# Sixteen-head attention steps: another order for the turned groups, and one copy moved from VectorE to ScalarE

## The reference, cut to what matters

```
scores = (q @ k.T) / sqrt(8)          # 128 queries x K keys; K = 120 (L1) or 128 (MLA)
scores = where(mask, -big, scores)    # a key mask in L1, causal in MLA
attn   = softmax(scores)              # over the keys
out    = attn @ v                     # 8 channels for each head, 16 heads side by side
y      = out.reshape(128, 128) @ w_o  # then the residual is added
```

## Time and profile before

| | |
|---|---|
| median of three runs | 1278.69 us |
| the profiled execution, its own time | 1280.42 us |
| its span, first to last instruction | 1278.9 us |
| TensorE matmul busy | 1221.2 us (95%) |
| VectorE busy | 936.8 us (73%) |
| ScalarE busy | 797.5 us (62%) |
| GpSimd busy | 585.1 us (46%) |
| mean granted TensorE clock | 0.981 |

### The profile page before, as it was taken

One profiled execution on the slowest core, in us unless ns is written; L12 is line 12 of the kernel. 1 busy time (PEld: TensorE's weight loads), 2 busy tenths in 40 slices (PEclk: granted clock), 3 DMA queues, 4 the chain that ended last, 5 costly groups with the idle time before them and its releaser, 6 DMA issues.

```text
span 1278.9 us, 38214 instructions
## 1 busy us (share of the span) xinstructions
PE 1221.2 (95%) x13719; PEld 874.3 (68%) x13719; DVE 936.8 (73%) x2049; ACT 797.5 (62%) x2101; POOL 585.1 (46%) x675
## 2 busy tenths in 40 slices
PE   4899999999999995998999999999999989999996
PEld 1566666666666664447888788788888767777774
DVE  7767766777667764579999999999999965344331
ACT  2687788878877783225877787767666733333331
POOL 5476666566665663414333423353233234333442
PEclk9999999999999998998999999999999999999998
DMA  9000000000000000000000002000000000000000
GB/s 225 14 2 2 0 0 0 0 0 0 0 0 0 1 1 5 0 0 12 10 10 10 11 8 72 3 4 1 0 0 0 1 1 9 9 8 8 8 16 10
DMA packets 22742, 14.74 MB, mean 12 GB/s; under 512 B 6378, under 2 KB 21610, under 8 KB 22540
## 3 DMA queue, kind: packets, MB, share of 16 engines
q1 hardware_dynamic: 22520, 13.75, 4.3%
q10 hardware_dynamic: 148, 0.01, 0.0%
HBM read 11.66 MB, written 2.10 MB: 11 GB/s over the span
## 4 chain that ended last, share of the span: by engine, by line
PE 40%; issue 10%; POOL 5%; DVE 3%; POOLq 0%; ACT 0%; DVEq 0%
PE psum L1580 10%; PE psum L1591 5%; PE psum L1567 5%; POOL pair_acc L2310 4%; PE psum L1594 4%; PE psum L998 2%; PE psum L2090 2%; PE psum L2100 2%; PE psum L1005 2%; PE psum L1562 2%; PE psum L1546 1%; PE psum L1548 1%; PE psum L1547 1%; PE psum L1602 1%; POOL pair_acc L2304 1%
## 5 line engine op out<-in xcount | busy, mean ns | idle before, releaser
L715 POOL TENSOR_TENSOR r_norm<-ssm,mhalf 128x24 f32<-128x24 f32 x32 | 134.9, 4215 | 156.9 <-DVE ssm L619 156.8
L1948 POOL TENSOR_TENSOR pair_QX<-pair_qT,own_slots 128x512 f32<-128x512 f32 x64 | 66.6, 1040 | 248.4 <-ACT pair_qT L1679 236.0
L2156 ACT ACTIVATE pair_hid<-psum 128x512 f32<-128x512 f32 x128 | 76.4, 597 | 141.3 <-PE psum L2090 141.3
L1580 PE MATMUL psum<-ident,pair_probs 128*120 128x128 f32 (+1 forms) x1024 | 153.9, 283 | 0.4 <-ACT pair_probs L1694 0.2
L541 ACT ACTIVATE l_probs<-psum,l_n_max 128x248 f32<-128x248 f32 x256 | 117.2, 482 | 57.9 <-DVE l_n_max L637 57.9
L2310 POOL TENSOR_TENSOR pair_acc<-pair_acc,pair_prod 128x512 f32<-128x512 f32 x64 | 81.2, 1269 | 140.0 <-DVE pair_prod L2269 140.0
L1694 ACT ACTIVATE pair_probs<-psum,pair_n_max 128x120 f32<-128x120 f32 (+1 forms) x512 | 137.7, 380 | 10.8 <-DVE pair_n_max L1748 5.7
L2100 PEld LDWEIGHTS psum<-w,pair_hid 128*128 128x128 f32 x1024 | 123.1, 192 | 26.8 <-issue 26.8
L2269 DVE TENSOR_TENSOR pair_prod<-psum,pair_combine 128x512 f32<-128x512 f32 x64 | 44.2, 691 | 129.7 <-PE psum L2100 129.5
L1515 ACT COPY pair_probsT<-psum 120x512 f32<-120x512 f32 (+1 forms) x128 | 78.7, 615 | 84.7 <-PE psum L1580 84.7
L1580 PEld LDWEIGHTS psum<-ident,pair_probs 128*120 128x120 f32 (+1 forms) x1024 | 109.4, 140 | 31.1 <-ACT pair_probs L1694 12.3
(11 more groups left out here) (294 smaller groups left out, 2922.9 us busy)
## 6 DMA issues: line engine op xcount, KB each, us to landing
X<-x_in SPq DMA_DIRECT2D x8, 256.0 KB, 6.2
out_dram<-pair_acc SPq DMA_DIRECT2D x32, 64.0 KB, 1.5
CT<-ctx_in SPq DMA_DIRECT2D x8, 240.0 KB, 6.6
pair_cT<-ctxT_in SPq DMA_DIRECT2D x32, 60.0 KB, 1.8
w<-w_in SPq DMA_DIRECT2D x1, 1024.0 KB, 5.4
wm<-wm_in SPq DMA_DIRECT2D x1, 768.0 KB, 7.3
wp<-wp_in SPq DMA_DIRECT2D x1, 768.0 KB, 8.7
wkv<-wkv_in SPq DMA_DIRECT2D x1, 512.0 KB, 5.0
```

What stands on the lines that cost most here:

```text
L715: pool.tensor_tensor(r_norm[:, :], ssm[:, :], mhalf[:, 0:3 * H], ALU.pow).then_inc(s["norm_inverted"], 1)
L1580: tr = pe.transpose(psum[0:K, 4 + g % 2, j * P:(j + 1) * P], probs[par][:, 4 * g + j, 0:K], ident[:, :])
```

## The change

TensorE's order becomes: turn the input of n+1; project n-2; turn group 3 of n-1; project q, k, v; turn group 2 of n-1; multiply groups 0, 1, 2, 3 of n-1; search totals; scores of n+1; turn group 1 of n; turn group 0 of n. So across the end of a step the four turned groups 1, 0, 3, 2 follow each other, and nothing is turned between the products.

ScalarE copies group 1 too, which VectorE copied. The exponentials of heads 0 to 7 move from the end of `body(n-1)` to `body(n)` in two halves; between the halves stand the copy of q of n+1 and the copy of group 2 of n-1.

VectorE loses the copy of group 1. Its copy of group 3 moves from before the projection's addition to behind `shift_b`, and `shift_b` now follows `max_b` at once; the statistics come after the copy.

```diff
 # TensorE, body(n)
-                    turn_group(n - 1, 1 - par, 3, l1)
                     if not (early and n == -1):
                         turn_input(n + 1)
                     if not (isinstance(n, int) and n == PAIR + 1):
                         project(n - 2, l1)
-                    turn_group(n - 1, 1 - par, 2, l1)
+                    turn_group(n - 1, 1 - par, 3, l1)
                     if isinstance(n, int) and n == PAIR:
                         pe.wait_ge(a_exp_done, PAIR)
                         moe["turn_first"](pe)
                     project_qkv(n + 1, 1 - par, l1)
+                    turn_group(n - 1, 1 - par, 2, l1)
...
                     multiply_v(n - 1, 1 - par, 0, l1)
                     multiply_v(n - 1, 1 - par, 1, l1)
-                    turn_group(n, par, 1, l1)
                     multiply_v(n - 1, 1 - par, 2, l1)
                     multiply_v(n - 1, 1 - par, 3, l1)
...
                     scores(n + 1, 1 - par, l1)
                     if early and n == -1:
                         find_logits()
+                    turn_group(n, par, 1, l1)
                     turn_group(n, par, 0, l1)
 # ScalarE
-                def exp_a(n, par, l1):
+                def exp_a(n, par, l1, some):
                     if there(n):
                         K = keys(n, l1)
                         wait(act, max_a_taken, n + 1)
                         wait(act, turned[1], n - 1)
-                        for h in range(8):
+                        wait(act, turned[0], n - 1)
+                        for h in some:
...
-                        e.then_inc(a_exp_done, 1)
+                        if some.stop == 8:
+                            e.then_inc(a_exp_done, 1)
 # ScalarE, body(n)
+                    exp_a(n, par, l1, range(0, 4))
                     copy_q(n + 1)
                     copy_group(act.copy, act, n - 1, 2, l1)
+                    exp_a(n, par, l1, range(4, 8))
                     copy_k(n + 1, 1 - par, l1)
...
+                    copy_group(act.copy, act, n, 1, l1)
                     copy_group(act.copy, act, n, 0, l1)
-                    exp_a(n + 1, 1 - par, l1)
 # VectorE, body(n)
                         copy_input(dve, n + 1, l1)
-                    copy_group(dve.tensor_copy, dve, n - 1, 3, l1)
...
                     add_projection(n - 2, l1)
                     max_b(n, par, l1)
+                    shift_b(n, par, l1)
+                    copy_group(dve.tensor_copy, dve, n - 1, 3, l1)
                     take_stats(n - 2, l1)
-                    shift_b(n, par, l1)
...
-                    copy_group(dve.tensor_copy, dve, n, 1, l1)
                     copy_values(dve.tensor_copy, dve, n + 1, 1 - par, l1)
```

## The result

The changed kernel takes 1293.54 us in the median of four runs (1293.49 to 1294.72); the kernel before, run beside it, 1279.61 (1275.88 to 1281.24, four runs). The ratio is 1.0117, with a 95% interval of 1.0098 to 1.0135: slower by 1.2%, where 0.4% was forecast. The profiled execution's span went from 1278.9 to 1291.9 us, +13.0.

A forecast was written before the change was run, and what follows sets the result against it. Two routes of one length, VectorE's and TensorE's, were taken to bound the MLA step. It grows from 6.76 to 6.90 us: +4.5 in 32 steps, L1 nothing, edges +0.3; +4.8 on 1278.69 gives 1283.5, range 1273 to 1295.

The forecast's parts named there:

- steps 2 to 5 of the sum: MLA step from `max_b` through group 3's copy and product 3 to `max_a`: 1.24, 1.12, 0.73, 0.78, 0.21, 0.98, 0.21 us.
- the 0.03 that the prediction added because two routes must be in: At `max_a`, VectorE's and TensorE's routes must both have arrived: 0.03 us added, taking the MLA step from 6.87 to 6.90.
- the wide range: Whole kernel's time, for 8 in 10: 1273 to 1295 us.
- the range of the forecast's own mechanism: Whole kernel's time if VectorE's wait for product 3 sets the step: 1278 to 1291 us, chance 0.64.
- the edges: Steps 17 (search's extra VectorE work, at most -0.6 us) and 64 (group 2's turn delayed, at most +1.1): +0.3 together.
- the addition's 0.26 in step 1: MLA step: VectorE's addition starts 0.26 us after the input copy, which starts 1.14 after `max_a`; `max_b` follows 0.20 later.
- Totals lengthen TensorE's route by 0.28 before and after alike: L1 steps with the search's totals: 0.28 us longer than other L1 steps, unaffected by the change, so L1 costs nothing.
- A free wait on the own engine: VectorE, `shift_b` behind `max_b`: waiting costs nothing, 0.11 us less in 64 steps, -7.0, giving 1276.5 us; chance 0.07.
- TensorE's run binds: TensorE's own work sets the step, 6.37 us MLA and 6.32 L1: -0.39 in 64 steps, -25, giving 1254; chance 0.15.
- ScalarE late: ScalarE's second half of the exponentials delays the bias: 0.24 us in 64 steps, +15 on the forecast, 1299; chance 0.11.
- The clock: TensorE rests about 0.5 us a step and its granted clock falls: at 0.85, +0.6 in 64 steps, about 1322; chance 0.03.

The follow-up runs named there:

- the first experiment: Changed kernel with VectorE's copy of group 3 moved between `max_b` and `shift_b`: 1278.54 us, ratio 1.0002 to the kernel before.

## Why the prediction was right in kind and short in size

- **What takes the step over: right.** `shift_b` at 1.25 behind `max_b` (forecast 1.24), 0.73 from group 3's copy to product 3, 0.78 to `copy_values`, then 0.21, 0.98, 0.21: as in steps 2 to 5 of the sum but for `shift_b`, 1.14 where 1.12 was forecast. `copy_values` waits 0.64 for L1594, the weight loads 0.67 for VectorE's copy; 0.6 and 0.5 were forecast. That the written-out step hits 6.90 is in part luck: the 0.03 that the prediction added because two routes must be in is not seen (VectorE goes on from `copy_values` at its own cost), and 0.01 of `max_b` and 0.02 of `shift_b` stand in its place.
- **The size.** 1293.54 lies inside the wide range but outside the range of the forecast's own mechanism, 1278 to 1291: +4.8 was forecast and +13.9 measured. The two failures below come to 3.2 and 6.6 of step time, and the edges gave 1.8 back.
- **What failed in the MLA: the addition's 0.26 in step 1.** I took it from the row of group 3's copy, which followed the input copy there; the addition stood behind that 0.60 copy, where nothing of its own lateness could show. In looped steps it starts 0.36 behind the input copy (mean; 911.70 - 911.35 = 0.35 above), the input copy 0.03 later than forecast and `max_b` 0.01: about 0.15 in 22 steps, 3.2 us. The 0.03 lay open in the trace of before: the input copy started 1.19 behind `max_a` in every second looped step there, and the prediction read one with 1.14. Written-out steps have 0.26 and 6.90. The last loop written out gives these 0.15 back, and the L1 steps show 6.81 and 6.70 in the same way. A looped addition's row shows no sizes of its inputs and a written-out one does, so its place in X comes from the loop's counter; whether that makes it late was not tried by itself. Why a looped instruction issues late stays open.
- **What failed in L1: "Totals lengthen TensorE's route by 0.28 before and after alike".** The prediction followed ScalarE for the scores, but not the third trial, which the totals need and which stands behind all that the change put on ScalarE. It ends at 658.10 + 0.23 = 658.33, and the totals start at 658.38. 15 steps, +6.6 us. The experiment with the early trial gives 4.8 of it back; the rest is the loop's lateness, and with the loops written out too the steps are back at 6.98.
- **Edges, too small**: the two steps of the search's extra work gained 1.8 where at most 0.6 was allowed. In the first (8.39 to 7.65) VectorE rests nowhere in the trace of before, so the copy taken off it counts there. The second (9.31 to 8.23) gained at least in part for a reason that the prediction does not have. TensorE's wait for the input copy there, before and after, and the stretch behind it before (columns as in the earlier trace rows):

```profile
709.81 0.49 PE L1546 MATMUL psum<-pair_zT,l_wq 128*128 128x128 f32 x2 [1.36 <-DVE pair_zT L1506]
```

```profile
713.09 0.49 PE L1546 MATMUL psum<-pair_zT,l_wq 128*128 128x128 f32 x2 [0.91 <-DVE pair_zT L1506]
```

```profile
711.00:712.00 1.00, 1.00 (x24) 0.92 (x26) 1.00 (x3) 1.00 (x4) 1.00 (x2) 0.50 0.00 0
```

  Behind the rest of 1.36 the granted clock fell to 0.50, the lower level, and group 1's turn and the products ran in that stretch; after the change it stayed at 1.00 through this step. What the clock cost there and what the order cost was not separated.
- **The rivals.** A free wait on the own engine: `shift_b` starts 0.03 behind the end of `max_b` (911.91 + 1.22 to 913.16), and filling that place gave 0.13. The Trainium skill, "VectorE: DVE Perf Modes", section "The DRAIN you can't avoid", measured no extra cost for a semaphore behind each of eight copies; the trace disagrees here too. TensorE's run binds: its condition, an early copy of group 3, is the first experiment, and it takes ScalarE's order as well to come near (6.55, not 6.37). ScalarE late: it came, but through the third trial and the totals and not through the exponentials that the rival names; 7.43 - 6.98 = 0.45 in 15 steps, the loop's part included. The clock: 1.00 over the MLA stretch, although TensorE's weight loads rest 0.67 in each step. The Trainium skill, "TensorE: Matmul & The Clock Gate", section "A second HAM failure mode: psum-queue depth-cycling", tells of a kernel in which short rests between matmul groups made the clock swing; no run here shows that for these steps.

## What to carry to other kernels

When a copy is moved so that an engine hands work over and next needs it back, its whole trip is on the path, and work taken off that engine was worth nothing here wherever it had to wait; move the copy up until other work covers the trip. When work is put on an engine, follow everything queued behind it to its own readers, the rare ones too: the steps with totals, 15 in one half, lost as much as 22 looped steps of the other. Take a price from a row with the same predecessor and, where steps are both looped and written out, from the same kind of step.

## What the runs showed of the hardware

A step run by the loop took 7.03 to 7.06 where the same step written out took 6.90, and 6.81 where it took 6.70. Before the change both kinds took about 6.75; there the addition followed the 0.60 copy. Behind `max_b`'s 1.21 the looped step is nearly as short as the written-out one, too (6.77 and 6.84 against 6.77), so a longer instruction ahead seems to cover the late issue. A VectorE instruction that reads the one right before it starts 0.03 behind its end, where one that does not starts 0.08 before; an independent instruction between them gave 0.13 of a step back. TensorE's granted clock fell to 0.50 behind one rest of 1.36 in the kernel before and behind one of 1.36 in the kernel with all steps written out.
